# The leaves' fourth weight part of the second layer as high and low parts, the low part made on GpSimd

## What is computed

```python
leaf = node - NN
h = act(jnp.einsum('bsd,bsdl->bsl', x, w1[leaf]) + b1[leaf])   # w1: (256, 1024, 16)
return jnp.einsum('bsl,bsld->bsd', h, w2[leaf]) + b2[leaf]     # w2: (256, 16, 1024)
```

## Time and profile before

| | us |
|---|---|
| median of 3 runs | 2379.18 (2377.16 to 2383.56) |
| the profiled execution | 2381.19 |
| its span from first to last instruction | 2379.4 |
| units 0 to 23 (k, q, v leaves) | 1202 to 1573 |
| units 24 to 31 (f leaves) | 1651 to 1766 |

### The profile page before, as it was taken

How to read it: one execution, slowest core, us unless ns; L and a number is a source line. 1 busy time by engine, 2 the same in 40 slices (tenths; PEclk the granted TensorE clock), 3 DMA queues, 4 the chain that set the end, 5 groups by cost and what they waited for, 6 DMA issues and landing times.

```text
span 2379.4 us, 31156 instructions
## 1 busy us (share of the span) xinstructions
PE 2322.5 (98%) x11941; PEld 1909.9 (80%) x11941; DVE 1409.4 (59%) x2469; ACT 853.4 (36%) x1057; POOL 244.2 (10%) x248
## 2 busy tenths in 40 slices
PE   7999999999999999999999999999999999999998
PEld 6888998888888888888877777888768889887666
DVE  7876453233333333345799887657885423558877
ACT  4323231111111212122257776643754222234442
POOL 2101320000000000011111111100111110202000
PEclk9999999999999999999999999999999999999999
DMA  6246723522132312134799999875985422355885
GB/s 183 73 106 158 156 79 120 138 95 85 49 97 63 98 51 83 47 112 137 255 307 324 354 353 333 276 210 171 345 306 164 143 80 71 89 183 179 303 286 167
DMA packets 168591, 406.27 MB, mean 171 GB/s; under 512 B 69550, under 2 KB 69840, under 8 KB 168413
## 3 DMA queue, kind: packets, MB, share of 16 engines
q1 hardware_dynamic: 143964, 338.41, 43.9%
q0 software_dynamic: 17584, 49.57, 7.2%
q10 hardware_dynamic: 6864, 15.88, 2.4%
HBM read 359.96 MB, written 56.76 MB: 175 GB/s over the span
## 4 chain that ended last, share of the span: by engine, by line
PE 86%; DVE 9%; DMA 3%; ACT 1%; issue 1%; DVEq 0%; SPq 0%; ACTq 0%; POOLq 0%
PE PS L322 17%; PE PS L324 17%; PE PS L323 17%; PE PS L1223 8%; PE PS L990 5%; PE PS L593 2%; DVE low L314 2%; PE PS L1926 2%; PE PS L1516 2%; PE PS L1933 2%; PE PS L1935 2%; PE PS L1934 2%; PE PS L341 2%; PE PS L2438 2%; DMA raw<-in_L_ffn_f_w 1%; PE PS L2380 1%
## 5 line engine op out<-in xcount | busy, mean ns | idle before, releaser
L314 DVE TENSOR_TENSOR low<-raw,high 128x1024 fp32r<-128x1024 f32 x473 | 569.4, 1241 | 121.8 <-ACT high L302 117.6
L302 ACT ACTIVATE high<-raw 128x1024 fp32r<-128x1024 f32 x476 | 484.4, 1056 | 299.6 <-PE PS L324 207.4
L322 PE MATMUL PS<-high,xt_high 128*128 128x512 f32 x1280 | 505.9, 395 | 3.4 <-DVE low L314 1.4
L324 PE MATMUL PS<-high,xt_low 128*128 128x512 f32 x1280 | 500.2, 391 | 0.0
L323 PE MATMUL PS<-low,xt_high 128*128 128x512 f32 x1280 | 499.7, 390 | 0.0
L322 PEld LDWEIGHTS PS<-high,xt_high 128*128 128x128 f32 x1280 | 241.2, 188 | 55.9 <-issue 2.7
L324 PEld LDWEIGHTS PS<-high,xt_low 128*128 128x128 f32 x1280 | 240.8, 188 | 51.1
L323 PEld LDWEIGHTS PS<-low,xt_high 128*128 128x128 f32 x1280 | 241.1, 188 | 48.7
L1247 ACT ACTIVATE y_high<-PS 125x512 fp32r<-125x512 f32 x80 | 47.8, 598 | 490.6 <-PE PS L324 490.6
L1258 DVE TENSOR_TENSOR y_low<-PS,y_high 125x512 fp32r<-125x512 f32 x80 | 55.3, 692 | 273.6 <-ACT y_high L1247 273.6
L1223 PE MATMUL PS<-y_high,a_kind 125*125 125x512 f32 x400 | 158.4, 396 | 0.0
(11 more groups left out here) (566 smaller groups left out, 3849.9 us busy)
## 6 DMA issues: line engine op xcount, KB each, us to landing
raw<-in_L_ffn_ew SPq DMA_DIRECT2D x96, 512.0 KB
raw<-in_L_gnn_weight SPq DMA_DIRECT2D x64, 512.0 KB
raw<-in_L_ffn_k_w SPq DMA_DIRECT2D x64, 512.0 KB, 9.1
raw<-in_L_ffn_q_w SPq DMA_DIRECT2D x64, 512.0 KB
raw<-in_L_ffn_v_w SPq DMA_DIRECT2D x64, 512.0 KB
raw<-in_L_ffn_f_w SPq DMA_DIRECT2D x64, 512.0 KB, 15.1
adjacency<-a_stage SPq DMA_DIRECT2D x10, 1120.0 KB
a_kind<-adjacency POOLq DMA_DIRECT2D x8, 1367.2 KB, 8.4
```

Source lines behind the costliest of these rows:

```text
L302: a.e.activation(high_of(i)[:, 0:w], RAW[PLACE_OF[i]][:, 0:w], ACT.Copy).then_inc(*a.step(part_high, 1, [("high", i)]))
L314: v.e.tensor_tensor(LOW[p][:, 0:w], RAW[p][:, 0:w], high_of(i)[:, 0:w], ALU.subtract).then_inc(*v.step(signal, 1, [("low", i)]))
L322: p.e.matmul(dst, xh[:, kt, xs], wh[:, c], start=first and j == 0, stop=False)
L324: ins = p.e.matmul(dst, xl[:, kt, xs], wh[:, c], start=False, stop=last and j == len(kts) - 1)
```

## The change

The fourth part of Wf2 leaves the list WHOLE for all 32 units, and is split as the first three are. Its high part is made by ACT. Its low part is made by POOL, as the first thing of POOL's step for a unit, ahead of the scatter. ht_high and ht_low grow from three to four column blocks, ht_whole and its copy on ACT go, and PE's second(n) has 24 split matmuls and no unsplit ones. The order of everything else stays.

```diff
-    WHOLE = [parts[3] for parts in Wf2.values()] + [part for x in range(8) for part in (We1[x][3], We2[x][2], We2[x][3])]
+    FOURTH = [parts[3] for parts in Wf2.values()]
+    WHOLE = [part for x in range(8) for part in (We1[x][3], We2[x][2], We2[x][3])]
...
     def low_on_gpsimd(i):
-        return i in (123, 124, 125)
+        return i in (123, 124, 125) or i in FOURTH
...
             for k, part in enumerate(Wf2[GROUP[n]]):
-                if k == 3:
-                    p.wait_ge(at("raw", part), at("hidden whole", n))
-                    for h in range(2):
-                        c = slice(512 * h, 512 * h + 512)
-                        ins = e.matmul(bank(5 + h), HTW[i][:, :], RAW[PLACE_OF[part]][:, c], start=False, stop=False)
-                    ins.then_inc(*p.mark("used", part))
-                    continue
                 p.wait_ge(at("high", part), at("low", part))
...
-                e.activation(HTW[n % 2][:, :], bank(4)[:, 384:512], ACT.Copy).then_inc(*a.mark("hidden whole", n))
-                e.activation(HTH[n % 2][:, :, :], bank(4)[:, 0:384].rearrange("p (k c) -> p k c", k=3), ACT.Copy).then_inc(*a.mark("hidden high", n))
+                e.activation(HTH[n % 2][:, :, :], bank(4).rearrange("p (k c) -> p k c", k=4), ACT.Copy).then_inc(*a.mark("hidden high", n))
...
-                e.tensor_tensor(HTL[n % 2][:, :, :], bank(4)[:, 0:384].rearrange("p (k c) -> p k c", k=3), HTH[n % 2][:, :, :], ALU.subtract).then_inc(*v.mark("hidden low", n))
+                e.tensor_tensor(HTL[n % 2][:, :, :], bank(4).rearrange("p (k c) -> p k c", k=4), HTH[n % 2][:, :, :], ALU.subtract).then_inc(*v.mark("hidden low", n))
...
     def leaves_gpsimd(g, run, begun, between):
         for n in range(run.first, run.end + 1):
             u = n - run.first
+            if u:
+                low_parts(g, Wf2[GROUP[n - 1]][3] + 1)
             if n == run.kept:
                 clear_rows(g, n)
```

More of the change, by code:

```diff
@@ L1798, in program @@
     HM = [place(f"h_masked{i}", [128, 512], F32, R0 + 16384 + 2048 * i) for i in range(2)]
-    HTH = [place(f"ht_high{i}", [128, 3, 128], F32R, R0 + 20480 + 4096 * i) for i in range(2)]
-    HTL = [place(f"ht_low{i}", [128, 3, 128], F32R, R0 + 20480 + 4096 * i + 2048) for i in range(2)]
-    HTW = [place(f"ht_whole{i}", [128, 128], F32, R0 + 20480 + 4096 * i + 1536) for i in range(2)]
+    HTH = [place(f"ht_high{i}", [128, 4, 128], F32R, R0 + 20480 + 4096 * i) for i in range(2)]
+    HTL = [place(f"ht_low{i}", [128, 4, 128], F32R, R0 + 20480 + 4096 * i + 2048) for i in range(2)]
     YO = [place(f"y_out{i}", [128, D], F32, R0 + 28672 + 4096 * i) for i in range(2)]
```

## The result

The changed kernel takes 2389.65 us, the median of 6 runs (2386.11 to 2392.70); the kernel before, run beside it, 2378.17 (6 runs). The ratio is 1.0046, with a 95% interval of 1.0036 to 1.0056: **11 us slower**. The forecast was 2383.5 in a range of 2374 to 2395, with 0.55 for "no change that can be told" and 0.38 for slower. The range holds the time; the likeliest case was the wrong one, and the loss is more than twice the +4.3 us that was forecast.

The account below looks back on a forecast made before the run. PE's time was taken to be on the path, with a second limit close behind that differs by stage. Terms +2.4 (k), 0 (units 7 to 16), -2.4 (v), +4.3 (f) gave +4.3 us: median 2383.5, range 2374 to 2395.

Parts of the forecast that it names:

- no change that can be told: Whole kernel: median between 2372.0 and 2386.3 us, within 0.3% (7.1 us) of before; chance 0.55.
- The mechanism: In the 32 units, a VectorE instruction with two SBUF inputs stands still while GpSimd runs, losing up to 2.3 us.
- PE's gain of 0.34 us per unit: Six split matmuls (1.38 us) replace one whole part (1.72 us) in each of 32 units; at most 10.9 us.
- ACT at nothing: ACT's added work, about +0.9 us per unit, costs nothing, except where raw parts come just in time.
- Stage k (+2.4): Units 0 to 6: stalls of 1.9 us in two units and 0.5 in two, less PE's gain: +2.4 us.
- the end of +9.6 given for k: Upper end for units 0 to 6, if every unit pays in full: 105.7 us of DVE work in 96.1.
- Units 7 to 16 (0): End of k, q, first of v: late raw-part landings take PE's 3.4 us gain; 0, ends -1 and +4.2.
- v (-2.4): Units 17 to 23: DVE has 28.6 us idle, so PE's gain comes through: -2.4 us, ends -2.4 and 0.
- f (+4.3): Last stage: DVE lag of 6.8 us, less 1.8 for low parts made ahead and 0.7 PE gain: +4.3 us.
- Unit 24's lag: First unit of f: 12.07 us busy of 13.1, so its added 2.4 leaves a DVE lag of 1.3 us.
- DVE pays in full: Rival, everywhere: POOL's part always falls inside DVE's low parts, 2.43 us per unit; 2391 to 2397 us, chance 0.24.

Follow-up runs that it names:

- no_low: Changed kernel with GpSimd's fourth low part left out, TensorE's middle matmul taking the high part a second time: 2373.78 us, ratio 0.9977.
- fill_three: Changed kernel with three GpSimd zero fills, one behind the other, in place of its subtraction in the 32 units: 2372.95 us, ratio 0.9984.

## Why the prediction was right or wrong

- **The mechanism: right**, place and sign. GpSimd's low parts collide with VectorE's, TensorE waits at the second layer's matmuls, VectorE's mean rises (forecast from 1241 toward 1400; 1306), GpSimd's are lengthened, and it is their reads that do it. A full collision costs VectorE about 2.2 us, where 2.3 was taken. (One reading behind it is loosely put: of the two low parts from 1063.46 it is the delay that reaches to GpSimd's end at 1065.01; the pair itself ends at 1067.22.) What was wrong is how often it is paid, and so the size of the sum: +10.9 us for +4.3.
- **PE's gain of 0.34 us per unit: right** where VectorE has time. In the trace of after, units 6 to 8 come 0.27, 0.44 and 0.34 us sooner each, and 21 to 23 0.49, 0.39 and 0.38.
- **ACT at nothing: right** by no_low and fill_three, but for raw parts that come just in time, as the prediction said (0.55 us once in fill_three). The 3.6 us for high parts in the list above bear the wrong name. One of the two longest, 1.61 us, ends at 1686.49. GpSimd's part ran to 1685.27, VectorE's second low part, which stood behind it, to 1686.34, and the second layer's high parts had been made by 1682.5:

```profile
1681.79 5.69 DVE L315 TENSOR_TENSOR low<-raw,high 128x1024 fp32r<-128x1024 f32 x3
```
```profile
1682.59 2.68 POOL L315 TENSOR_TENSOR low<-raw,high 128x1024 fp32r<-128x1024 f32 x1 [0.23 <-ACT high L303]
```
```profile
1679.57 2.94 ACT L303 ACTIVATE high<-raw 128x1024 fp32r<-128x1024 f32 x3
...
1686.49 0.47 PE L1926 MATMUL PS<-high,ht_high 128*128 128x512 f32 x1 [1.61 <-ACT high L303]
```
- **Stage k (+2.4): mis-sized, the main miss.** Forecast: 1.9 us in units 3 and 5, 0.5 in 0 and 1, none in 2, 4 and 6. The trace: stalls of 1.61, 1.71 and 1.91 us in units 1, 3 and 5. The price of a collision was right; the number of them wasn't. VectorE is caught in full in units 0, 1, 3, 4 and 5, not in two units. Unit 1 passes it on to TensorE, since VectorE there begins three low parts together too. Unit 0 lost 1.4 us on the lag, unit 4 another 0.5, by b_parts that VectorE then makes late (4.5 us of waits in all, in the list above), a follower that the forecast didn't price. Measured +4.8 alone, +8.4 in the trace up to the end of k; the end of +9.6 given for k holds both.
- **Units 7 to 16 (0): the number near, the reason wrong, so its nearness is luck.** In the changed kernel no landing took PE's gain; only kernels that run ahead of before, as no_low and fill_three, lose some of it there. In the trace of the changed kernel it arrived in most of these units, and stalls took it back (lag -0.7 in q); alone q costs 2.6 +- 2.2. The rising lag from k did not shrink either, and ACT's wait for raw parts near 1440 stayed (10.3 us in 11 waits before, 11.1 in 11 after):

```profile
ACT high L303 <- DMA raw<-in_L_ffn_v_w: 11.1, 11, 3.0
```
- **v (-2.4): right as far as can be told.** PE is busy 94.72 of 96.2 us in its window, without waits for low parts, though with one of 0.86 us for b_parts; alone -0.5 +- 2.2.
- **f (+4.3): right mechanism, a little small**; alone +5.9 +- 2.3. VectorE is full (86.05 of 87.0 us), as the sum of work had said (88.8 in 83.3). Unit 24's lag in that sum should be 1.4 us, not 1.3 (12.07 + 2.4 - 13.1).
- **The rival "DVE pays in full"** (2391 to 2397) was nearer in time than the forecast: 2389.65 is 1.4 us below its range and 6.2 above 2383.5. Its mechanism was not met: VectorE lost (1306 - 1241) ns x 473 = 31 us, 0.96 per unit, not 2.43, since much of GpSimd's time fell beside waits and PSUM reads of VectorE, in q and v above all. That it came so near in time is thus luck in part.
- **The chances.** All four terms were too low: k's, q's, v's and f's by 2.4, 2.6, 1.9 and 1.6, those of v and f within their intervals. In k and v I had looked at where VectorE waits and called those units free. The terms share one unknown, how often GpSimd falls among VectorE's low parts, so their errors are likely to add; with that seen, slower would have had more than 0.38. The range held the time only because its upper end was made for the rival.

## What to carry over

Before giving GpSimd work that reads SBUF, list what VectorE does in the microseconds after the moment it will be released: if those are instructions with two SBUF inputs that TensorE waits for, the engine "idle six sevenths of the time" isn't free, and giving the work to the busy VectorE itself can be cheaper (here by 12 us). In these runs GpSimd's writes cost VectorE's two-input instructions nothing, so fills are what to give it. Compare two traces only after listing the half-speed stretches of each: here they hid up to 6.8 of 11.5 us and made one look like an absorbing DMA wait.

## What the runs showed of the hardware

- Three fills by GpSimd, 3.0 us of writes, beside three two-input subtractions of VectorE: 0 us lost. One GpSimd subtraction of 2.4 us in the same place: 2.2 us lost.
- A GpSimd tensor_scalar with one SBUF input (2.79 us alone for 128x1024) kept VectorE's two-input instruction for 0.84 us only, and went on beside the next one. The Trainium skill, SBUF — State Buffer, "Who interferes with whom", calls the shared port pair an exclusive lock and, for VectorE's two-port modes, gives it to whoever issued first for the whole instruction; the subtraction fits that (VectorE's part lasts 3.42 us, to 1.1 us after its end), this one doesn't, and the measurement decides.
- The same 128x1024 float32 tile takes GpSimd 0.96 us to fill, 2.39 to 2.43 to subtract and 2.79 to multiply by a constant, each undisturbed; VectorE's subtraction takes 1.17 when three stand back to back.
- TensorE's granted clock: stretches at 1.2 GHz in a trace that is otherwise at 2.4. In ten of fourteen traces one begins in or just after TensorE's wait of 2.3 to 3.0 us for q_rows; in the changed kernel's trace that wait was 2.5 us and none followed.
